# The ten x tiles of a graph kernel's front stage: plain transfers of SyncE or row gathers of GpSimd

## What is computed

```
x = layernorm(x + gcn(x, src, dst, W, b))            # + self loops, degree-normalised
h = elu(rgat(x, W1, q1, k1, b1, heads=4))            # xr = x @ W[r] for each of 3 relations,
y = rgat(h, W2, q2, k2, b2, heads=1)                 # softmax over the edges of each dst node
out = layernorm(x + y)

# gcn:
deg = segment_sum(1, col); dinv = rsqrt(deg)
out = segment_sum((x @ W)[row] * dinv[row] * dinv[col], col) + b
```

## Time and profile before

| | us |
|---|---|
| median of 3 runs | 1905.66 |
| lowest, highest | 1905.25, 1909.72 |
| the profiled execution | 1900.88 |
| its span, first to last instruction | 1899.1 |
| mean granted TensorE clock | 0.926 of full |

### The profile page before, as it was taken

One profiled execution on the slowest core, in us unless ns is written; L12 is line 12 of the kernel. 1 busy time (PEld: TensorE's weight loads), 2 busy tenths in 40 slices (PEclk: granted clock), 3 DMA queues, 4 the chain that ended last, 5 costly groups with the idle time before them and its releaser, 6 DMA issues. The chain is left out here.

```text
span 1899.1 us, 25964 instructions
## 1 busy us (share of the span) xinstructions
PE 1628.5 (86%) x9203; PEld 1363.3 (72%) x9203; DVE 1216.3 (64%) x1945; ACT 593.9 (31%) x927; POOL 238.8 (13%) x171
## 2 busy tenths in 40 slices
PE   5998879788796999899899899422999999999997
PEld 4674445454386999899799799201788888888787
DVE  6447666656249989989999998065532433344554
ACT  2331222232123543543353354101421322133332
POOL 1000000000030003003101200001520232033201
PEclk8989889898898999899899899665999999999998
DMA  7761134423566656563655552364300121012211
GB/s 214 259 235 71 35 77 101 91 78 73 130 204 183 199 197 192 171 234 104 204 169 203 173 148 87 115 183 127 111 24 16 49 61 32 10 56 70 81 46 47
DMA packets 153369, 230.72 MB, mean 121 GB/s; under 512 B 36797, under 2 KB 101439, under 8 KB 152745
## 3 DMA queue, kind: packets, MB, share of 16 engines
q1 hardware_dynamic: 151860, 225.25, 40.1%
q10 hardware_dynamic: 1396, 3.96, 0.6%
HBM read 184.06 MB, written 45.10 MB: 121 GB/s over the span
## 5 line engine op out<-in xcount | busy, mean ns | idle before, releaser
L1576 PE MATMUL ah_ps<-ah_xr,ah_T 125*125 125x194 f32 x2400 | 405.8, 332 | 40.2 <-issue 37.1
L1576 PEld LDWEIGHTS ah_ps<-ah_xr,ah_T 125*125 125x125 f32 x2400 | 402.4, 191 | 42.6 <-issue 37.9
L1408 ACT ACTIVATE ah_T<-ah_T,ah_kq 125x625 f32<-125x625 f32 x240 | 195.9, 817 | 223.0 <-DVE ah_T L1506 223.0
L1129 PE MATMUL att_ps<-att_AH,att_sH 125*128 125x500 f32 (+1 forms) x540 | 193.6, 358 | 34.9 <-POOL att_AL L950 23.0
L1489 DVE CUSTOM_DVE_ANT_0 ah_dump<-ah_krow,ah_gap 125x1250 bf16<-125x1250 f32 x120 | 206.1, 1781 | 15.7 <-DMA ah_krow<-ah_d_k 15.6
L1506 DVE SCALAR_TENSOR_TENSOR ah_T<-ah_rows,ah_k_rest 125x625 f32<-125x625 f32 x240 | 211.1, 881 | 0.4
L1513 DVE SCALAR_TENSOR_TENSOR ah_T<-ah_T,ah_cnt 125x625 f32<-125x625 f32 x240 | 192.6, 802 | 19.2 <-DMA ah_cnt<-d_C 17.6
L1129 PE MATMUL att_ps<-att_AH,att_sL 125*128 125x500 f32 (+1 forms) x540 | 193.6, 359 | 0.0
L1129 PE MATMUL att_ps<-att_AL,att_sH 125*128 125x500 f32 (+1 forms) x540 | 192.2, 356 | 0.0
L607 PE MATMUL fr_ps<-fr_col_hot,fr_row_hot 125*128 x516 | 122.1, 364 | 44.0 <-DVE fr_col_hot L401 37.4
L950 POOL TENSOR_TENSOR att_AL<-att_T,att_AH 125x500 fp32r<-125x500 f32 (+1 forms) x90 | 102.4, 1139 | 407.2 <-ACT att_AH L888 407.2
(11 more groups left out here) (199 smaller groups left out, 2360.8 us busy)
## 6 DMA issues: line engine op xcount, KB each, us to landing
ah_gap<-d_gap SPq DMA_DIRECT2D x120, 312.5 KB, 3.5
ah_cnt<-d_C SPq DMA_DIRECT2D x240, 156.2 KB, 3.8
ah_rows<-ah_d_rows SPq DMA_DIRECT2D x24, 625.0 KB, 5.2
fr_raw<-in_w SPq DMA_DIRECT2D x36, 384.0 KB, 6.1
d_gap<-fr_gap SPq DMA_DIRECT2D x30, 312.5 KB, 2.5
d_C<-fr_C SPq DMA_DIRECT2D x15, 625.0 KB, 10.3
st_gap<-d_gap SPq DMA_DIRECT2D x30, 312.5 KB, 3.4
ah_krow<-ah_d_k SPq DMA_DIRECT2D x4, 1875.0 KB
```

Of the source, the lines that this page charges most:

```text
L1129: mm = pe.matmul(ps[:, c, 0:gn], a[:, j, cols], b, start=(j == 0 and k == 0), stop=(j == NT - 1 and k == 2))
L1408: act.activation(T[:, g % TR], T[:, g % TR], ACT.Exp, bias=k_slope[:, j, h, r:r + 1]).then_inc(e_made, 1)
L1576: mm = pe.matmul(o, T[:, g % TR, t * P:(t + 1) * P], xr[:, r, j], start=(first and t % 2 == 0), stop=final, skip_group_check=True)
```

## The change

The ten tiles of x are no longer issued by SyncE. GpSimd makes a table of row numbers with an iota (`x_row`, one column a tile, one number a partition) and issues ten indirect transfers, each of which reads one row number a partition and brings that row of x. Two stand at the head of GpSimd's list, ahead of ident, the other eight behind `big` and ahead of the fill of gap_rows; from tile 6 on each waits for the turn of the tile six places before it. They count on new semaphores `x_in`, and so the counts of raw_in for w1 and w2 tiles start from zero. The bytes, the slots and all other work are the same.

```diff
+        x_row = sb("x_row", [CH, NT], I32)
...
+        x_in = [S(f"x_in{i}") for i in range(RG)]
...
                 s = e % RG
-                if e < NT:
-                    n0, nn = x_rows(e)
-                    sp.dma_start(raw[0:nn, s], x[n0:n0 + nn, :]).then_inc(raw_in[s], 16)
...
-            for e in range(RG):
-                load(e)
             for h in range(2):
...
-            for e in range(RG, NT):
-                load(e)
             sp.wait_ge(span_out, 32)
...
+            def gather_x(i):
+                n0, nn = x_rows(i)
+                if i >= RG:
+                    pool.wait_ge(x_turned, i - RG + 1)
+                pool.indirect_dma_start(raw[0:nn, i % RG], None, x, bass.IndirectOffsetOnAxis(ap=x_row[0:nn, i:i + 1], axis=0))\
+                    .then_inc(x_in[i % RG], 16)
+
+            iota(x_row[:], [[CH, NT]], 0, 1).then_inc(x_row_made, 1)
+            pool.wait_ge(x_row_made, 1)
+            for i in range(2):
+                gather_x(i)
             pool.memset(ident[:], 0.0).then_inc(made, 1)
...
             pool.memset(big[:], -NO_EDGE).then_inc(iotas, 1)
+            for i in range(2, NT):
+                gather_x(i)
             pool.wait_ge(iotas, 7)
             pool.memset(gap_rows[96:CH], -NO_EDGE).then_inc(gap_filled, 1)
...
-                v.wait_ge(raw_in[e % RG], 16 * (e // RG + 1))
+                v.wait_ge(raw_in[e % RG], 16 * len([o for o in range(NT, e + 1) if o % RG == e % RG]))
...
             def turn_x(i):
...
-                pe.wait_ge(raw_in[i % RG], 16 * (i // RG + 1))
+                pe.wait_ge(x_in[i % RG], 16 * (i // RG + 1))
```

More of the change, by code:

```diff
@@ L156, in front @@
         made, ident_ready, identb_ready, gap_filled = S("made"), S("ident"), S("identb"), S("gap_filled")
+        x_row_made = S("x_row_made")
         x_turned, x_copied = S("x_turned"), S("x_copied")
@@ L204, in load @@
                 s = e % RG
-                if e < NT:
-                    n0, nn = x_rows(e)
-                    sp.dma_start(raw[0:nn, s], x[n0:n0 + nn, :]).then_inc(raw_in[s], 16)
[L208 to L212, removed]
+                u = (e - NT) // 2
+                w = w1 if (e - NT) % 2 == 0 else w2
+                r, c = u // FC, u % FC
+                sp.dma_start(raw[:, s], w[r, c * CH:(c + 1) * CH, :]).then_inc(raw_in[s], 16)
             def split_out(u):
@@ L463, in split_high @@
                 e = w1_entry(u)
-                act.wait_ge(raw_in[e % RG], 16 * (e // RG + 1))
+                act.wait_ge(raw_in[e % RG], 16 * len([o for o in range(NT, e + 1) if o % RG == e % RG]))
                 if u >= 2:
@@ L576, in turn_w @@
                 b = 2 * (u % 2)
-                pe.wait_ge(raw_in[e % RG], 16 * (e // RG + 1))
+                pe.wait_ge(raw_in[e % RG], 16 * len([o for o in range(NT, e + 1) if o % RG == e % RG]))
                 if u >= 2:
```

## The result

The changed kernel takes 1916.43 us (median of 4 runs, 1914.91 to 1919.38) against 1906.43 us for the kernel before on the same chip (4 runs): ratio 1.0052, interval 1.0033 to 1.0070. It is 10 us slower. The profiled execution took 1915.67 us with a span of 1913.9 us.

A forecast was written before the change was run, and what follows sets the result against it. TensorE was taken as the bound from 40.2 us. Earlier x gains 3.5 us at full clock, 1.5 us with half clock charged: 1905.66 - 1.5 = 1904.2 us (1899.4 for the profiled execution); range 1899 to 1917.

The forecast's parts named there:

- What bounds the kernel: TensorE from 40.2 us on; moving the start of the first transform (40.12 us) should move the whole rest.
- step 3: GpSimd's added iota and ten gathers: issuing one gather taken as 1.1 us, kept within 0.4 to 3.3 us.
- Rival B: Dear gathers on GpSimd: at 3.3 us each the degree work ends at 51.6 to 53.6 us, +12 us, 1918 us; chance 0.10.
- step 4: Start of GpSimd's queue: io_colf ready near 4.9 us; VectorE's one-hot tiles shift by 0, bounds -1.3 and +3.1 us.
- d: Shift of both VectorE one-hot tiles, taken as 0, with -1.3 and +3.1 us as bounds.
- +3.1: Bound on VectorE's one-hot chain: that many us later if gathers of tiles 2 to 5 each held VectorE 1.1 us.
- step 5: Front, x loads: gathers issued by 14.7 us, x landed by about 22 us, tile 9 turned by 20 to 23 us.
- Rival A: Gathers locked out by VectorE's two long one-hot instructions: transform(0) at 53.3 us, +13 us, 1919 us; chance 0.16.
- the lock: GpSimd gathers and VectorE's two-SBUF-input instructions excluding each other for whole instructions: +13 us, +11 with the clock kept up; chance 0.16.
- Step 2: Tiles 6 to 9 leave SyncE's queue; GpSimd sends each once the tile five places earlier is turned.
- step 6: Degree matmuls' second half waits for dst_hot[1] at 31.88 us; ends at 36.6 at full clock, 38.7 charged: gain 1.5 us.
- the slow restart: TensorE after some 5 us idle before the second degree half: 4.1 us at half clock, 6.8 us instead of 4.75.

The follow-up runs named there:

- the one of SyncE: Bounded kernel before, with SyncE's four late x tiles issued ahead of the span bounds, q1 and k1, no gathers: 1917.06 us, ratio 1.0049, first transform at 38.44 us.

## Why the prediction was wrong

The forecast was a gain of 1.5 us, the measurement is a loss of 10. The measured time is inside the stated range, by its upper edge, only because the range was stretched to 1917 us for the rivals' sake; the forecast's own bounds ended at 1909. It is the case that I gave 16 in 100.

- **What bounds the kernel: right.** 10.65 us at the first transform, 10.0 us in the medians. What the stretches behind it add in the profiled execution, 4.1 us, is no more than executions of one kernel differ by.
- **The price of a gather (step 3): right.** I took 1.1 us; alone it takes 0.94 to 1.16. Rival B falls.
- **The start of GpSimd's queue and the shift of VectorE's chain (step 4): right in number, by luck in part.** io_colf ended at 5.46 us (4.70 + 0.76), where I had 4.9; the first long one-hot instruction started at 10.89 us instead of 10.82, so d = 0.07 against 0. But I had balanced the memset's wait against a gather's, and no gather held VectorE: the cast of io_colf ended at 6.05 us, 0.6 us earlier than before, and VectorE then waited 0.50 us for the id lists to land. The +3.1 that I kept as a bound was not touched.
- **"Gathers 2 to 9 follow from about 5.9 us with at least g each: 14.7 us" (step 5): this step failed.** It put the wait for the port at nothing. Two gathers took 10.18 us each, the last one ended at 36.5 us instead of 14.7, and tile 9 was turned at 41.5 us instead of 20 to 23. I had both facts in hand, the exclusion in the earlier trace rows and 21 us of two-input instructions without a gap in the earlier trace rows, and put the case at 0.16 because a gather "reads only one number a partition". How much it reads doesn't matter; that it reads at all does: each held gather ended 0.8 us after the end of the VectorE instruction beside it. The runs with one input in PSUM and with plain transfers show it from both sides: take away VectorE's second SBUF input, or the gather's read, and no gather or transfer is held for 10 us.
- **Rival A's own sum** gave +13 us with the slow clock and +11 with the clock kept up; it was 10.65 at that point. It had three gathers to run after 33 us, as measured (33.07, 34.31, 35.57 us), and the turned tile at 41.7, measured 41.5. The degree work took its full pace, 4.80 and 4.75 us. But two of A's parts were wrong and cancelled: it let tile 5 slip in before the long instructions, where that gather was held for 10.18 us, and it had a gather push the second one-hot tile to 33 us, where that tile ended at 31.95. So A was right in mechanism, its size came out near in part by luck, and its chance was set too low.
- **"x has landed by about 22 us" (step 5): wrong also without the lock.** With gathers that nothing holds, the last tile was turned at 31.0 us, with q1 and k1 out of the way at 27.4, with plain transfers at 25.6. I added up bytes at the best rate, but the tiles wait for one another through the ring: with the keys in PSUM tile 9 was issued at 19.0 us, when tile 3 was turned, and then needed 10.7 us to land. (Step 2 says five places earlier; it is six, the length of the ring.) So with nothing held for long the gather kernel of this form was hardly faster at the first transform (39.41, 40.51 and 41.75 us in the three kernels that still have q1 and k1 early) than the kernel before (40.12 to 41.63), and little of the forecast gain would have come even without the lock.
- **What early x is worth (step 6): right in size.** 36.6 to 38.7 us; measured 36.55, 37.20 and 38.44 in the three kernels with waits for halves whose last tile was turned at 25.6 to 27.4 us. The wait for dst_hot[1] that the step is built on came in one of them, with plain transfers (1.03 us before 32.52 us); the slow restart came in the one of SyncE, in the other half.

## What to carry to other kernels

Before a gather (or another GpSimd instruction that reads SBUF) is put on a path, look for VectorE instructions with two SBUF inputs in the same stretch and take their length, not GpSimd's, as its price: each gather can cost a whole one (10.18 us here). If they can't be moved, cut them into pieces about as long as a gather, put one input into PSUM, or use a transfer that needs no list. And where loads compete, put the tiles that the next engine waits for ahead of the weights that are needed later, in the queue itself: here that, together with matmuls that follow the pieces, brought the first transform 8.1 us forward, where the best kernel that only changed the issuing engine (plain transfers of GpSimd) brought it 2.9 us forward (37.20 against 40.13).

## What the runs showed of the hardware

- A gather excludes a two-input VectorE instruction for its read at most, not for its whole length: a held gather ends 0.8 us after the VectorE instruction, when the next one already runs, and that one isn't delayed (it starts 10.49 us after the one before it, with gathers and without).
- GpSimd issues a plain transfer of 128 rows in 0.54 us, a gather of as many in 0.95 us and starts the next one 0.3 us later.
- The granted clock is shown as 1.00 through the first 40 us of the changed kernel, and yet the six transposes of a tile take 1.51 to 1.54 us in each of its first six tiles, where they take 0.84 us in the earlier trace rows (12 in 1.65 us in the kernel with all x first); in the kernel before the record falls to 0.50. I can't tell from these traces whether the record misses a step there. It touches no step above: the degree matmuls of the changed kernel ran at 4.80 us.
- The addition, 200 bounds instructions on two engines' sequencers with an offset beside them, cost 10 to 15 us, as much as the change under study or more.
